# Last stage with rows loaded in place and the norm two steps behind; the experts' narrow product in column groups

## The chip, the cores and the metric

The kernel runs on one core of one Trainium2 chip. The core has TensorE (PE in the profile: matmuls, with its weight loads as PEld), VectorE (DVE), ScalarE (ACT), GpSimd (POOL), SyncE (SP, which here only issues DMAs) and 16 DMA engines. The metric is the device time of one execution in microseconds (us). 0.2% of it is about 8 us.

## What is computed

A decoder layer of three sublayers, each with a residual and a layer norm, in fp32, for x of 8 batches x 512 tokens x 512. The first two are a self-attention with relative positions and a causal cross-attention. The third is a soft mixture of experts: 16 slots gather from the tokens, each slot passes through its own expert, and the tokens read the slots back. Cut to what matters here:

```python
q = broadcast(slot_query)                       # (8, 16, 512)
o = q + _mha(q, x, x, d_Wq, ...)                # slots gather from tokens
h = _layernorm(o.reshape(8, 16, 1, 512), e_ln_g, e_ln_b)
u = silu(einsum('besd,edf->besf', h, e_W1) + e_b1)      # d = 512, f = 2048, e = 16
g = silu(einsum('besd,edf->besf', h, e_Wg) + e_bg)
y = einsum('besf,efd->besd', u * g, e_W2) + e_b2
o = o + y
out = _mha(x, o, o, c_Wq, c_bq, c_Wk, c_bk, c_Wv, c_bv, c_Wo, c_bo)   # tokens read 16 slots
x = _layernorm(x + out)
```

## The kernel before

The program is a row of stages, each a function with a block of instruction streams, one for each engine, that wait for each other by semaphores; between stages all engines meet and the stage's semaphores are cleared. The last two stages are touched by the change.

**`experts`** (line 1547). A loop over 16 experts, with batch (8) as the free size of the slots. The weights of an expert are three tiles of 4 MB (`w1`, `wg`, `w2`), each with two buffers; SP issues them in this order, a buffer as soon as the product that read it is done (`d_wide`, `d_narrow`). PE does for each of `w1` and `wg` a wide product: 16 matmuls with 32 columns of slots as stationary and 512 columns of weights moving, four at a time into four groups of 32 partitions of `ps_u` (line 1618). The result is copied, transposed (1626), and DVE and ACT make silu and the product `prod` (1666). The narrow product (1634) has `prod`, 128x8, as stationary and a 128x512 piece of `w2` moving, 16 matmuls that all sum into the same 8 partitions of `ps_y`. DVE copies `ps_y` to `y` (1671), and POOL's queue stores it (1695). Behind the last expert SP also loads what the last stage needs into the buffers that come free: four 1 MB weights into `w1`, four small tiles into `wg`, and there also `xT0` and `x0`, the first batch of tokens, transposed and as rows (1600 to 1606).

**`slots_to_tokens`** (line 1717). Its SP loads `y_all` (1773). DVE clears `kd` and `vd` (1876, 1877), adds `y` and `b2` to `o` (1880, 1882), fills `bq` (1884), and copies `oT` (1886) after PE's transposes of `o`. PE projects `oT` to keys and values (1793), DVE spreads them by heads into `kd` and `vd` (1893), and 18 rounds on PE fold the query weights into the keys and the output weights into the values (1807 to 1814), copied out by DVE and ACT in turn (`fold_out`). So each batch needs only: `scores` (1825, `xT` against `a`), a softmax over 16 slots for each head (`soft_in` 1907 to 1915 on DVE, the exponential 1993 on ACT, `soft_out` 1920 to 1924 on DVE), `turn` (1836, transposes), the copy `pt` (1990 on ACT), `mix` (1845, into `ps_o`), then `norm_in` (1932 adds `ps_o` to `h`, 1937 the statistics), `norm_scales`, `norm_out` and ACT's scaling of `h` (2000), and the store (1763).

Here `h = x + bo` is made by POOL (1974) from the loaded rows `x[j]` into `h[j]`, with two buffers of each. The loop's step `s` does on PE `scores(s)`, `turn(s-1)`, `mix(s-1)`; on DVE `soft_in(s)`, `soft_out(s)`, `norm_in(s-1)` to `norm_out(s-1)`; on SP `load(s+1)` and then `store(s-1)`. `load` issues `xT` and `x` of a batch once `e_scored` and `e_xb` say that the buffers are read. Instructions of an engine run in the order written, so whatever stands behind a wait waits too. `loop` (1116) writes out two steps, a loop of two steps and the last ones.

Of the kernel before, what the change touches and what calls it, by code (L numbers as in the profile page):

```python
# [6 lines left out]
ALU = mybir.AluOpType  # L7
# [4 lines left out]
P = 128  # L12
T4 = S // P
K4 = E // P
H = 16
# [1531 lines left out]
def experts(nc, dr, sem, first, keep):  # L1547


    with ExitStack() as ctx:  # L1550
# [14 lines left out]
        prod = sb("prod", [P, FC, B])  # L1565
# [3 lines left out]
        ps_t = ps("ps_t", [P, 2, 512])  # L1569
        ps_y = ps("ps_y", [B, 512])  # L1570
# [4 lines left out]
        def _(sp):  # L1575
# [20 lines left out]
            weights, xT0, x0, rows, cols = token_tiles(first)  # L1596
# [43 lines left out]
        def _(dve):  # L1640
            def step(e, j):
# [24 lines left out]
                dve.tensor_tensor(prod[:, :, :], act_e[:, 0, :, :], act_e[:, 1, :, :], ALU.mult)\  # L1666
# [4 lines left out]
                dve.tensor_copy(y[32 * j:32 * j + B, :], ps_y[:, :]).then_inc(sem["d_y"], 1)  # L1671

            dve.wait_ge(sem["d_const_in"], 16)
# [28 lines left out]
D_SEMS = ["d_" + n for n in ["sp_waited", "pool_waited", "wide", "narrow", "w1_in1", "wg_in1",  # L1702
# [4 lines left out]
TOKEN_SEMS = ["e_const_in", "e_in0"]  # L1707


def slots_to_tokens(nc, dr, sem, first, keep):  # L1710


    with ExitStack() as ctx:
# [17 lines left out]
        x = [x0, sb("x1", [P, T4, E])]  # L1731
        h = [sb(f"h{i}", [P, T4, E]) for i in range(2)]
# [3 lines left out]
        st = [sb(f"st{i}", [P, T4, 16]) for i in range(2)]  # L1736
# [6 lines left out]
        const_in = 16 * 9  # L1743
        block = ctx.enter_context(nc.Block())

        @block.sync
        def _(sp):
# [3 lines left out]
            def load(b, j):  # L1751
                if not early(b, 2):
                    sp.wait_ge(sem["e_scored"], b - 1)
                    settle()
                    sp.wait_ge(sem["e_xb"], b - 1)
                    settle()
                sp.dma_start(xT[j][:, :, :], dr["x2T"](b)).then_inc(sem[f"e_in{j}"], 16)
                sp.dma_start(x[j][:, :, :], dr["x2"](b)).then_inc(sem[f"e_in{j}"], 16)

            def store(b, j):  # L1760
                sp.wait_ge(sem["e_normed"], b + 1)
                settle()
                sp.dma_start(dr["out"](b), h[j][:, :, :]).then_inc(sem[f"e_stored{j}"], 16)

            def step(s, j):
                if inside(s, -1, B):
                    load(s + 1, 1 - j)
                if inside(s, 1, B):
                    store(s - 1, 1 - j)

            for j in range(2):
                sp.sem_inc(sem[f"e_stored{j}"], 16)
            sp.dma_start(y[:, :], dr["y_all"]).then_inc(sem["e_const_in"], 16)
            loop(sp, B, step, 1)
            for j in range(2):
                sp.wait_ge(sem[f"e_stored{j}"], 8 * B + 16)

# [5 lines left out]
        def _(pe):  # L1783
# [35 lines left out]
            def scores(b, j):  # L1819
                pe.wait_ge(sem[f"e_in{j}"], (b - j) * 16 + 32)  # L1820
                if not early(b, 1):
                    pe.wait_ge(sem["e_biased"], b)
                for t in range(T4):
                    for k in range(K4):
                        mm = pe.matmul(ps_s[:, t // 2, (t % 2) * HS:(t % 2 + 1) * HS], xT[j][:, k, t * P:(t + 1) * P],  # L1825
                                       a[:, k, b, :, :].rearrange("p m n -> p (m n)"),
                                       start=(k == 0), stop=(k == K4 - 1))
                mm.then_inc(sem["e_scored"], 1)

            def turn(b, j):  # L1830
                pe.wait_ge(sem["e_probs"], b + 1)
                if not early(b, 1):
                    pe.wait_ge(sem["e_pt"], b)
                for i in range(2):
                    for t in range(T4):
                        mm = pe.transpose(ps_t[:, i, t * P:(t + 1) * P], sc[j][:, t, i * P:(i + 1) * P], ident[:, :])  # L1836
                mm.then_inc(sem["e_turned"], 1)

            def mix(b, j):
                pe.wait_ge(sem["e_pt"], b + 1)  # L1840
                if not early(b, 1):
# [7 lines left out]
            def step(s, j):  # L1849
                if inside(s, 0, B):  # L1850
                    scores(s, j)
                if inside(s, 1, B):
                    turn(s - 1, 1 - j)
                    mix(s - 1, 1 - j)
# [3 lines left out]
            loop(pe, B, step, 1)  # L1858
# [16 lines left out]
        def _(dve):  # L1875
            dve.memset(kd[:, :, :, :, :].rearrange("p m b h s -> p (m b h s)"), 0.0).then_inc(sem["e_kd"], 1)
            dve.memset(vd[:, :, :, :, :].rearrange("p m b h s -> p (m b h s)"), 0.0).then_inc(sem["e_kd"], 1)
# [4 lines left out]
            dve.tensor_tensor(o[:, :], o[:, :], b2[:, :], ALU.add).then_inc(sem["e_o"], 1)  # L1882
            for m in range(K4):
# [14 lines left out]
            def groups(j):  # L1898
                return sc[j][:, :, :].rearrange("p t (h s) -> p (t h) s", s=NS)

            def soft_in(b, j):

                dve.wait_ge(sem["e_scored"], b + 1)
                if not early(b, 2):
                    dve.wait_ge(sem["e_turned"], b - 1)
                for u in range(2):
                    ins = dve.tensor_tensor(sc[j][:, 2 * u:2 * u + 2, :],
# [251 lines left out]
```

## Time and profile before

| what | value |
|---|---|
| median of 3 timed runs | 3957.59 us (3953.12 to 3958.68) |
| the profiled execution, as timed | 3950.47 us |
| its span in the profile | 3948.8 us |
| experts in it, from the first wide product | about 3222 to 3712 us |
| last stage in it | 3712 us to the end |
| PE busy | 3612.2 us (91%) |
| mean of what the DMA engines moved | 277 GB/s |

The rows further down come from the trace of that one execution. Times are us from the span's start. The windows view gives the busy time of each engine in a stretch, the clock that PE was granted (1.00 is 2.4 GHz), the busy share of the DMA engines and what they moved. The timeline gives for each instruction, or several of a line merged, its start, the time it covers, the engine and source line, the tiles written and read, and how long the engine stood idle before it and what released it. The chain is the row of work that ended last, followed back from the last instruction.

### The profile page before, as it was taken

How to read it: one execution, taken by the hardware profiler on the slowest of the kernel's cores; microseconds unless marked ns; L12 is line 12 of the kernel's file. 1: busy time of each engine (PE TensorE's matmuls, PEld its weight loads, DVE VectorE, ACT ScalarE, POOL GpSimd, SP SyncE). 2: the span in 40 equal slices, each digit the busy share in tenths (PEclk: the TensorE clock that was granted, in tenths of full speed). 3: DMA queues.
4: the chain of work that ended last, by engine and by line, in shares of the span. 5: the costliest groups of instructions: out<-in, count | busy, mean ns of one | idle time of the engine just before them, and what ended most of it. 6: DMA issues, size and time to landing. Idle time of an engine off the chain costs nothing. (4 is left out here: it accounts for less than half of the span.)

```text
span 3948.8 us, 65903 instructions
## 1 busy us (share of the span) xinstructions
PE 3612.2 (91%) x19712; PEld 2254.9 (57%) x19712; DVE 2163.0 (55%) x5872; ACT 1769.2 (45%) x3799; POOL 1822.9 (46%) x1652
## 2 busy tenths in 40 slices
PE   6999989999899999999888999999899977888686
PEld 4777767777677777777444555555455531122253
DVE  4666656666566666666685666666333321111355
ACT  4666556666566666665355555555121210000033
POOL 3666656666566666665326777777211000000112
PEclk8999999999999999999999999999999988889898
DMA  7999999999899999999783322222444249999623
GB/s 281 386 386 382 379 367 361 385 381 382 339 392 385 376 388 380 384 383 390 227 251 109 94 84 84 84 84 74 156 165 160 88 168 415 417 418 415 246 93 120
DMA packets 429721, 1091.94 MB, mean 277 GB/s; under 512 B 25152, under 2 KB 107584, under 8 KB 380224
## 3 DMA queue, kind: packets, MB, share of 16 engines
q1 hardware_dynamic: 412208, 1040.34, 70.5%
q10 hardware_dynamic: 16656, 47.19, 3.1%
q8 instruction: 161, 2.64, 0.3%
q14 instruction: 184, 1.51, 0.1%
q0 software_dynamic: 512, 0.26, 0.0%
HBM read 650.97 MB, written 436.73 MB: 275 GB/s over the span
## 5 line engine op out<-in xcount | busy, mean ns | idle before, releaser
L553 POOL TENSOR_SCALAR a_sc<-a_sc,a_inv 128x512 f32<-128x512 f32 x512 | 822.6, 1607 | 586.2 <-DVE a_inv L496 541.4
L505 DVE COPY a_pt<-a_ps_t 128x512 f32<-128x512 f32 x512 | 353.5, 690 | 545.6 <-PE a_ps_t L237 528.3
L1096 POOL TENSOR_SCALAR b_sc<-b_sc,b_inv 128x128 f32<-128x128 f32 (+3 forms) x512 | 546.3, 1082 | 179.3 <-DVE b_inv L1065 175.9
L375 ACT ACTIVATE a_stage_q<-a_ps_b 128x640 f32<-128x640 f32 x512 | 360.5, 704 | 586.1 <-PE a_ps_b L255 552.3
L1026 ACT ACTIVATE b_sc<-b_sc,b_mx 128x128 f32<-128x128 f32 (+3 forms) x512 | 282.0, 552 | 317.1 <-DVE b_mx L1059 316.8
L489 DVE CUSTOM_DVE_ANT_0 a_sc<-a_ps_s,a_rq 128x512 f32<-128x512 f32 x512 | 353.2, 690 | 76.4 <-PE a_ps_s L227 60.5
L365 ACT ACTIVATE a_sc<-a_sc,a_mx 128x512 f32<-128x512 f32 x512 | 370.0, 723 | 56.0 <-DVE a_mx L489 52.2
L375 ACT ACTIVATE a_stage_k<-a_ps_b 128x640 f32<-128x640 f32 x512 | 357.7, 699 | 0.0
L237 PEld LDWEIGHTS a_ps_t<-a_ident,a_sc 128*128 128x128 f32 x2048 | 247.5, 141 | 146.3 <-issue 140.4
L1059 DVE CUSTOM_DVE_ANT_0 b_sc<-b_ps_s,b_mask 128x128 f32<-128x128 f32 (+3 forms) x512 | 229.5, 488 | 164.8 <-PE b_ps_s L974 161.0
L237 PE MATMUL a_ps_t<-a_ident,a_sc 128*128 128x128 f32 x2048 | 308.9, 273 | 9.2 <-DVE a_pt L505 9.2
L227 PE MATMUL a_ps_s<-a_ident,a_rk 128*128 128x128 f32 x2048 | 307.9, 273 | 0.0
L324 PEld LDWEIGHTS a_ps_o<-a_okv,keep 128*128 128x128 f32 x2048 | 263.3, 191 | 76.4 <-issue 72.0
L1695 POOL DMA_DIRECT2D y<-d_y x16 | 8.5, 532 | 586.6 <-DVE d_y L1671 586.6
L227 PEld LDWEIGHTS a_ps_s<-a_ident,a_rk 128*128 128x128 f32 x2048 | 256.5, 141 | 37.9 <-issue 1.0
L275 PE MATMUL a_ps_c<-a_xT,keep 128*128 128x512 f32 x512 | 256.4, 605 | 22.1 <-DVE a_lo_q L459 12.1
L324 PE MATMUL a_ps_o<-a_okv,keep 128*128 128x128 f32 x2048 | 269.5, 276 | 1.6 <-ACT a_kv L397 1.6
L321 PE MATMUL a_ps_o<-keep,a_okv 128*128 128x512 f32 x512 | 265.8, 606 | 0.4 <-ACT a_kv L400 0.4
L960 PE MATMUL b_ps_q<-b_xT,keep 128*128 128x512 f32 x512 | 259.3, 610 | 6.8 <-PEq L2081 6.8
L225 PE MATMUL a_ps_s<-a_ks,a_qs 128*128 128x512 f32 x512 | 248.1, 485 | 17.4 <-issue 12.3
L1072 DVE COPY b_pt<-b_ps_t 128x128 f32<-128x128 f32 (+3 forms) x512 | 226.9, 485 | 63.7 <-PE b_ps_t L982 63.6
L1249 PE MATMUL f_ps_o<-keep,f_cT 128*128 128x512 f32 x512 | 231.5, 607 | 9.4 <-DMA f_x<-x 9.4
(207 smaller groups left out, 6335.4 us busy)
## 6 DMA issues: line engine op xcount, KB each, us to landing
band_q<-a_stage_q SPq DMA_DIRECT2D x128, 1280.0 KB, 7.0
band_k<-a_stage_k SPq DMA_DIRECT2D x128, 1280.0 KB, 10.0
a_rk<-band_k SPq DMA_DIRECT2D x128, 1024.0 KB, 12.6
a_rq<-band_q SPq DMA_DIRECT2D x256, 512.0 KB, 13.3
d_w<-in_e_W SPq DMA_DIRECT2D x24, 4096.0 KB, 42.8
d_wg<-in_e_Wg SPq DMA_DIRECT2D x16, 4096.0 KB, 28.4
keep<-in_e_W SPq DMA_DIRECT2D x8, 4096.0 KB, 36.1
a_okv<-in_b_wkv ACTq DMA_DIRECT2D x62, 512.0 KB, 7.9
```

Source lines behind the costliest of these rows:

```text
L227: mm = pe.matmul(out[:, r * P:(r + 1) * P], rk[h][:, r, t * P:(t + 1) * P], ident[:, :], is_transpose=True, start=False, stop=(r == T4 - 1))
L237: mm = pe.transpose(ps_t[:, r * P:(r + 1) * P], sc[i % SC][:, r * P:(r + 1) * P], ident[:, :])
L321: mm = pe.matmul(ps_o[:, :], okv[c][:, 0, n, :], oc[:, n, :], start=(n == 0), stop=(n == K4 - 1))
L324: mm = pe.matmul(ps_o[:, n * P:(n + 1) * P], oc[:, k, n * P:(n + 1) * P], okv[c][:, 1, k, :], start=(k == 0), stop=(k == K4 - 1))
L365: act.activation(sc[n][:, :], sc[n][:, :], ACT.Exp, bias=mx[:, n:n + 1], scale=-1.0, accum_out=sm[:, n:n + 1]).then_inc(sem["a_exped"], 1)
L375: act.activation(st[h % 2][:, t, :], src, ACT.Copy).then_inc(sem[f"a_{kind}_staged"], 1)
L489: dve.tensor_tensor_reduce(out=sc[n][:, :], in0=ps_s[i % 2][:, :], in1=rq[rn][:, i % 2, :], scale=-SCALE_A, scalar=BIG, op0=ALU.add, op1=A ...
L505: dve.tensor_copy(pt[:, h % 2, :, t * P:(t + 1) * P], ps_t[:, :].rearrange("p (r n) -> p r n", r=T4)).then_inc(sem["a_pt_out"], 1)
L553: pool.tensor_scalar(sc[n][:, :], sc[n][:, :], inv[:, n:n + 1], None, ALU.mult)\
L960: mm = pe.matmul(ps_q[:, :], wq[:, j % XP, k, :], xT[j // XP][:, k, :], start=(k == 0), stop=(k == K4 - 1))
L1026: act.activation(sc[j % 2][i][:, 0:width(i)], sc[j % 2][i][:, 0:width(i)], ACT.Exp, bias=mx[j % 2][:, i:i + 1], scale=-1.0, accum_out=sm[j ...
L1096: pool.tensor_scalar(sc[j % 2][i][:, 0:width(i)], sc[j % 2][i][:, 0:width(i)], inv[j % 2][:, i:i + 1], None, ALU.mult).then_inc(sem["b_nor ...
```

## The change

In `experts`: `prod` gets 32 columns for each piece, of which 8 are written and the rest are zero from a clear at the beginning. Each matmul of the narrow product writes one of four groups of 32 partitions of a new tile `ps_p`, by its piece `f`. DVE copies `ps_p` to `part`, and one more matmul with `select` (which sums the four groups' rows; made at the beginning from the identity) brings `ps_y`. The two loads of the first batch are taken out of the end of SP's stream.

In `slots_to_tokens`: the first batch is loaded right behind `y_all`. The clears of `kd` and `vd` and the filling of `bq` stand behind the copy of `oT`; POOL waits for `oT_ready` before its first add. Rows are loaded straight into `h`, which has three buffers, and POOL adds `bo` in place; a row load waits for the store that read the buffer. The norm of a batch is done two steps after its scores, in DVE ahead of `soft_in` (`norm_in`, `norm_scales`) and between `soft_in` and `soft_out` (`norm_out`). The turns stand between the two halves of the next batch's scores. All steps are written out.

```diff
@@ experts
-        prod = sb("prod", [P, FC, B])
+        prod = sb("prod", [P, FC, 32])
+        part = sb("part", [P, E])
+        select = sb("select", [P, B])
+        ps_p = ps("ps_p", [P, 512])
@@ sync
-            sp.dma_start(xT0, dr["x2T"](0)).then_inc(sem["e_in0"], 16)
-            sp.dma_start(x0, dr["x2"](0)).then_inc(sem["e_in0"], 16)
@@ tensor
                 if not early(e, 1):
-                    pe.wait_ge(sem["d_y"], e)
+                    pe.wait_ge(sem["d_part"], e)
                 for n in range(FC):
                     c, f = n // FQ, n % FQ
-                    mm = pe.matmul(ps_y[:, :], prod[:, n, :], w2[j][:, 4 * f + c, :], start=(n == 0), stop=(n == FC - 1))
+                    mm = pe.matmul(ps_p[32 * f:32 * f + 32, :], prod[:, n, :], w2[j][:, 4 * f + c, :],
+                                   start=(c == 0), stop=(c == FC // FQ - 1))
                 mm.then_inc(sem["d_narrow"], 1)
+                pe.wait_ge(sem["d_part"], e + 1)
+                if not early(e, 1):
+                    pe.wait_ge(sem["d_y"], e)
+                pe.matmul(ps_y[:, :], select[:, :], part[:, :], start=True, stop=True).then_inc(sem["d_added"], 1)
@@ vector
                 dve.wait_ge(sem["d_narrow"], e + 1)
+                if not early(e, 1):
+                    dve.wait_ge(sem["d_added"], e)
+                dve.tensor_copy(part[:, :], ps_p[:, :]).then_inc(sem["d_part"], 1)
+                dve.wait_ge(sem["d_added"], e + 1)
                 if not early(e, 2):
                     dve.wait_ge(sem[f"d_stored{j}"], (e - j) * 8)
                 dve.tensor_copy(y[32 * j:32 * j + B, :], ps_y[:, :]).then_inc(sem["d_y"], 1)
@@ slots_to_tokens
-        x = [x0, sb("x1", [P, T4, E])]
-        h = [sb(f"h{i}", [P, T4, E]) for i in range(2)]
+        h = [x0, sb("h1", [P, T4, E]), sb("h2", [P, T4, E])]
@@ sync
+            def load_xT(b):
+                if b >= 2:
+                    sp.wait_ge(sem["e_scored"], b - 1)
+                    settle()
+                sp.dma_start(xT[b % 2][:, :, :], dr["x2T"](b)).then_inc(sem[f"e_in{b % 2}"], 16)
+            def load_x(b):
+                if b >= 3:
+                    sp.wait_ge(sem[f"e_stored{b % 3}"], 16 * (b // 3))
+                    settle()
+                sp.dma_start(h[b % 3][:, :, :], dr["x2"](b)).then_inc(sem[f"e_x_in{b % 3}"], 16)
+            def step(s):
+                if s + 1 < B:
+                    load_xT(s + 1)
+                if s >= 2:
+                    store(s - 2)
+                if 1 <= s + 1 < B:
+                    load_x(s + 1)
             sp.dma_start(y[:, :], dr["y_all"]).then_inc(sem["e_const_in"], 16)
+            load_xT(0)
+            load_x(0)
@@ tensor
+            def step(s):
+                if s < B:
+                    scores(s, 0)
+                if 0 <= s - 1 < B:
+                    turn(s - 1)
+                if s < B:
+                    scores(s, 1)
+                if 0 <= s - 1 < B:
+                    mix(s - 1)
@@ vector
-            dve.memset(kd ...)
-            dve.memset(vd ...)
             dve.memset(eps[:, :], EPS).then_inc(sem["e_eps"], 1)
             dve.wait_ge(sem["e_const_in"], const_in)
             ...
+            dve.wait_ge(sem["e_oT_ready"], 1)
+            dve.tensor_copy(oT[:, :, :].rearrange("p k n -> p (k n)"), ps_t[:, 0, :]).then_inc(sem["e_oT"], 1)
+            dve.memset(kd ...)
+            dve.memset(vd ...)
             for m in range(K4):
                 dve.tensor_copy(bq[:, m, :], cols[:, 0, m:m + 1].to_broadcast([P, P])).then_inc(sem["e_bq"], 1)
-            dve.wait_ge(sem["e_oT_ready"], 1)
-            dve.tensor_copy(oT[:, :, :].rearrange("p k n -> p (k n)"), ps_t[:, 0, :]).then_inc(sem["e_oT"], 1)
             ...
+            def step(s):
+                if s >= 2:
+                    norm_in(s - 2)
+                    norm_scales(s - 2)
+                if s < B:
+                    soft_in(s)
+                if s >= 2:
+                    norm_out(s - 2)
+                if s < B:
+                    soft_out(s)
@@ gpsimd
-                    ins = pool.tensor_tensor(h[j][:, t, :], x[j][:, t, :], bo[:, :], ALU.add)
+                    ins = pool.tensor_tensor(h[b % 3][:, t, :], h[b % 3][:, t, :], bo[:, :], ALU.add)
...
             pool.wait_ge(sem["e_const_in"], const_in)
-            loop(pool, B, step, 0)
+            pool.wait_ge(sem["e_oT_ready"], 1)
+            for b in range(B):
+                add(b)
@@ scalar
+            def step(s):
+                if 0 <= s - 1 < B:
+                    turned_out(s - 1)
+                if s >= 2:
+                    std(s - 2)
+                if s < B:
+                    softexp(s)
+                if s >= 2:
+                    norm(s - 2)
```

## Rows read from the trace of the kernel before

**Rows 1.** Windows view: engines' busy us (instructions), PE's clock, DMA share, GB/s; experts.

```profile
3222.00:3712.00 490.00, 391.09 (x1664) 95.58 (x1664) 77.55 (x144) 17.49 (x33) 8.52 (x16) 0.89 1.01 409
```

**Rows 2.** Timeline, the last expert: start, us, engine, line, tiles, [idle before <-releaser].

```profile
3679.80 3.62 PE L1618 MATMUL d_ps_u<-d_wg,d_hs 128*32 128x512 f32 x32
...
3688.28 0.29 DVE L1666 TENSOR_TENSOR d_prod<-d_act_e 128x128 f32<-128x128 f32 x1
...
3690.14 15.96 PE L1634 MATMUL d_ps_y<-keep,d_prod 128*8 128x512 f32 x32 [5.25 <-DMA keep<-in_e_W]
...
3706.14 0.68 DVE L1671 COPY d_y<-d_ps_y 8x512 f32<-8x512 f32 x1 [17.57 <-PE d_ps_y L1634]
3707.43 0.52 POOL L1695 DMA_DIRECT2D y<-d_y  x1 [30.15 <-DVE d_y L1671]
```

**Rows 3.** Timeline, beginning of the last stage.

```profile
3712.86 1.76 DVE L1876 MEMSET e_kd<- 128x2048 f32 x1 [6.04 <-PEq L2081]
...
3715.35 5.83 POOL L1974 TENSOR_TENSOR e_h<-d_wg 128x512 f32<-128x512 f32 x4 [7.40 <-DMA e_y<-y]
3716.69 1.69 DVE L1880 TENSOR_TENSOR d_wg<-d_wg,e_y 128x512 f32<-128x512 f32 x1
...
3719.97 4.94 DVE L1884 COPY e_bq<-d_wg 128x128 f32<-128x128 f32 x4
3720.20 1.09 PE L1787 MATMUL e_ps_t<-d_ident,d_wg 128*128 128x128 f32 x4 [14.09 <-DVE d_wg L1882]
...
3730.89 1.10 DVE L1893 TENSOR_SCALAR e_kd<-e_ps_s,d_wg 32x128 f32<-32x128 f32 x3 [5.37 <-PE e_ps_s L1793]
```

**Rows 4.** Chain that ended last, in order of time: start, us, what; last stage.

```profile
3743.03 1.30 DVE e_a L1896 x2
...
3775.12 7.16 PE e_ps_s L1825 x32
...
3830.01 9.54 DMA d_wg<-x
...
3924.13 9.97 PE e_ps_o L1845 x16
3934.12 2.37 DVE e_h L1932 x2
...
3939.14 0.39 DVE e_st L1944 x4
```

**Rows 5.** Timeline, the first wide product of the experts.

```profile
3222.11 5.89 PE L1618 MATMUL d_ps_u<-d_w,d_hs 128*32 128x512 f32 x32 [2.25 <-DVE d_hs L1644]
```

**Rows 6.** Windows view, the first 3 us of the last narrow product.

```profile
3690.00:3693.00 3.00, 2.85 (x4) 0.51 (x5) 0.00 (x0) 0.00 (x0) 0.00 (x0) 0.50 1.04 384
```

**Rows 7.** Timeline by engine, first steps of the batch loop.

```profile
3790.72 1.04 PE L1836 MATMUL e_ps_t<-d_ident,e_sc 128*128 128x128 f32 x8
3792.87 7.13 PE L1845 MATMUL e_ps_o<-keep,e_pt 128*128 128x512 f32 x16 [1.11 <-ACT e_pt L1990]
...
3810.40 8.80 PE L1845 MATMUL e_ps_o<-keep,e_pt 128*128 x16 [2.61 <-ACT e_pt L1990]
...
3782.31 1.29 DVE L1907 TENSOR_TENSOR e_sc<-e_ps_s,e_cb 128x512 f32<-128x512 f32 x2 [8.80 <-PE e_ps_s L1825]
...
3789.14 1.22 DVE L1924 TENSOR_TENSOR e_sc<-e_sc,e_inv 128x1024 f32<-128x1024 f32 x1
...
3814.50 2.26 DVE L1924 TENSOR_TENSOR e_sc<-e_sc,e_inv 128x1024 f32<-128x1024 f32 x1
...
3806.42 2.93 ACT L2000 ACTIVATE e_h<-e_h,e_st 128x512 f32<-128x512 f32 x4 [0.65 <-DVE e_st L1953]
...
3814.41 5.91 POOL L1974 TENSOR_TENSOR e_h<-d_wg 128x512 f32<-128x512 f32 x4 [88.35 <-DMA out<-e_h]
...
3809.45 0.38 SPq L1763 DMA_DIRECT2D out<-e_h  x1
```

**Rows 8.** DMA issues, experts and beginning of the last stage: KB, us to landing.

```profile
e_x<-x SPq DMA_DIRECT2D x1, 1024.0 KB, 7.5
```

More of the change, by code:

```diff
@@ L1595, in _ @@
             loop(sp, NS, step, 0)
-            weights, xT0, x0, rows, cols = token_tiles(first)
+            weights, _, _, rows, cols = token_tiles(first)
             sp.wait_ge(sem["d_wide"], 2 * NS - 3)
@@ L1671, in step @@
                 dve.tensor_copy(y[32 * j:32 * j + B, :], ps_y[:, :]).then_inc(sem["d_y"], 1)
+            dve.memset(prod[:, :, :], 0.0).then_inc(sem["d_set"], 1)
+            dve.wait_ge(sem["d_set"], 1)
+            dve.tensor_reduce(select[:, :], ident[:, :].rearrange("p (f r) -> p r f", f=FQ)[:, 0:B, :], AX.X, ALU.add)\
+               .then_inc(sem["d_set"], 1)
+            dve.wait_ge(sem["d_set"], 2)
             dve.wait_ge(sem["d_const_in"], 16)
@@ L1699, in _ @@
                 pool.wait_ge(sem[f"d_stored{j}"], 8 * NS)
-D_SEMS = ["d_" + n for n in ["sp_waited", "pool_waited", "wide", "narrow", "w1_in1", "wg_in1",
+D_SEMS = ["d_" + n for n in ["set", "part", "added", "sp_waited", "pool_waited", "wide", "narrow", "w1_in1", "wg_in1",
                              "w2_in0", "w2_in1", "hs", "pre", "pre_g", "in", "turned", "prod", "y", "exp",
@@ L1735, in slots_to_tokens @@
         pt = sb("pt", [P, 2, S])
-        st = [sb(f"st{i}", [P, T4, 16]) for i in range(2)]
+        st = [sb(f"st{i}", [P, T4, 16]) for i in range(3)]
         eps = sb("eps", [P, 1])
@@ L1743, in slots_to_tokens, with steps @@
         const_in = 16 * 9
+        def steps(step):
+            for s in range(B + 2):
+                step(s)
         block = ctx.enter_context(nc.Block())
@@ L1817, in _, with scores, turn @@
                 mm.then_inc(sem["e_fold"], 1)
[L1819 to L1823, printed above, removed]
+            def scores(b, half):
+                if half == 0:
+                    pe.wait_ge(sem[f"e_in{b % 2}"], 16 * (b // 2) + 16)
+                    if b:
+                        pe.wait_ge(sem["e_biased"], b)
+                for t in (2 * half, 2 * half + 1):
                     for k in range(K4):
-                        mm = pe.matmul(ps_s[:, t // 2, (t % 2) * HS:(t % 2 + 1) * HS], xT[j][:, k, t * P:(t + 1) * P],
+                        mm = pe.matmul(ps_s[:, t // 2, (t % 2) * HS:(t % 2 + 1) * HS], xT[b % 2][:, k, t * P:(t + 1) * P],
                                        a[:, k, b, :, :].rearrange("p m n -> p (m n)"),
                                        start=(k == 0), stop=(k == K4 - 1))
-                mm.then_inc(sem["e_scored"], 1)
-            def turn(b, j):
+                if half:
+                    mm.then_inc(sem["e_scored"], 1)
+            def turn(b):
                 pe.wait_ge(sem["e_probs"], b + 1)
-                if not early(b, 1):
+                if b:
                     pe.wait_ge(sem["e_pt"], b)
@@ L1847, in mix @@
                 mm.then_inc(sem["e_mixed"], 1)
[L1849 to L1854, printed above, removed]
+            def step(s):
[7 more added lines that the diff above has]
+                    mix(s - 1)
             for j in range(2):
                 pe.wait_ge(sem[f"e_folded{j}"], len(rounds) // 2)
-            loop(pe, B, step, 1)
+            steps(step)
         def fold_out(e, parity, copy):
@@ L1923, in soft_out, with norm_in @@
                 dve.wait_ge(sem["e_inv"], b + 1)
[L1924 removed]
+                dve.tensor_tensor(groups(b), groups(b), inv[:, :].unsqueeze(2).to_broadcast([P, T4 * H, NS]),
                                   ALU.mult).then_inc(sem["e_probs"], 1)
[L1927 removed]
+            def norm_in(b):
                 dve.wait_ge(sem["e_mixed"], b + 1)
@@ L1931, in norm_in @@
                 for u in range(2):
-                    ins = dve.tensor_tensor(h[j][:, 2 * u:2 * u + 2, :], ps_o[u][:, :, :],
-                                            h[j][:, 2 * u:2 * u + 2, :], ALU.add)
+                    ins = dve.tensor_tensor(h[b % 3][:, 2 * u:2 * u + 2, :], ps_o[u][:, :, :],
+                                            h[b % 3][:, 2 * u:2 * u + 2, :], ALU.add)
                 ins.then_inc(sem["e_summed"], 1)
@@ new lines, in norm @@
+            def norm(b):
+                act.wait_ge(sem["e_scales"], b + 1)
+                for t in range(T4):
+                    ins = act.activation(h[b % 3][:, t, :], h[b % 3][:, t, :], ACT.Identity, bias=st[b % 3][:, t, 10:11],
+                                         scale=st[b % 3][:, t, 9:10])
+                ins.then_inc(sem["e_normed"], 1)
+            def step(s):
[7 more added lines that the diff above has]
+                    norm(s - 2)
@@ L2004, in _ @@
             act.wait_ge(sem["e_eps"], 1)
-            loop(act, B, step, 1)
-E_SEMS = ["e_" + n for n in ["sp_waited", "dve_waited", "scored", "xb", "in1", "normed", "stored0", "stored1",
+            steps(step)
+E_SEMS = ["e_" + n for n in ["sp_waited", "dve_waited", "scored", "xb", "in1", "x_in1", "x_in2", "normed", "stored0", "stored1", "stored2",
                              "o", "oT_ready", "oT", "kv_ready", "kd", "bq", "folded0", "folded1", "fold",
```

112 lines of the change are left out of this document (41 added, 71 removed).

## The prediction

> **What bounds the kernel now.** Every number is of one profiled execution: span 3948.8 us, 3950.47 us as timed; the three timed runs have a median of 3957.59. I take the change in the span off the median.
>
> First view: the stretches. The change touches only the last 727 us. In the experts (3222 to 3712) the DMA engines are busy all the time at 409 GB/s [rows 1]: 12.58 MB of weights per expert take about 30 us, and PE's narrow product starts when its `w2` lands [rows 2]. So nothing inside the experts is worth time; only what comes behind the last landing is. That is next [rows 2]: the last `w2` lands at 3690.14, the narrow product takes 15.96, `y` is copied by 3706.82, stored at 3707.43, and the last stage's first DVE instruction starts at 3712.86. All this is serial.
>
> Then the last stage's beginning [rows 3]: DVE clears `kd` and `vd`, adds `y` and `b2` to `o` and fills `bq` before it copies `oT`, so PE's projections start only 4.2 us after its transposes end, and DVE then waits 5.37 us for the first of them. POOL adds `bo` to the first two batches meanwhile, and DVE's adds and copies take as long as POOL's instructions.
>
> Last, the chain of the eight batches [rows 4]. Scores start at 3775.12 and the span ends at 3948.8: 173.7 us. In the chain PE's scores and mixes stand in series with DVE's `h` sums, ACT's norm and, from batch 3 on, a load (9.54 us in the row shown) issued only once the row store before it was let go by the norm. PE is not full; a dependency ring is the bound.
>
> **A. Narrow product in four column groups.** 16 matmuls 128x8 become 16 of 128x32 in four groups, the form of the wide product: as many instructions of 128x512, 3.62 us at the high clock [rows 2], 5.89 us for the first burst of the stage, after a stretch without PE work [rows 5]. The last narrow product started at granted clock 0.50, that is 1.2 GHz, after a stretch without PE work [rows 6]. I take 5.89. It may also start later: the last wide product was held by PE's own work and is now held by `wg`, which lands 10 us (4.19 MB at 409 GB/s) before `w2`, at 3680.0; plus 3.62 to 5.89, plus the 5.15 from its end (3683.42) to the end of `prod` (3688.57) gives 3688.8 to 3691.0 against the landing 3690.14. I take a start of 3690.6 and an end of 3696.5. Added: the copy of `part` (0.68 as `y`'s, 0.04 to start), one matmul of 128x512 with `select` (one of the 16 now takes 15.96/16 = 1.0; I take that, and 2.0 at the low clock, though the burst comes right before it), and `y`'s copy, unchanged, 0.72: 3699.0 against 3706.82. **Gain 7.8**; all at high clock 10.7, all low 6.6. The `prod` clear and `select`'s reduce at the stage's start lie under the weights' stream. The extra DVE and PE waits stand before nothing due: the next `w1` lands 10 us later.
>
> A page of the Trainium skill, "TensorE: Matmul & The Clock Gate", section "HAM oscillation — how this bites in real kernels", speaks against this change: short bursts behind DMA waits all start at the low clock. The clock row agrees for the narrow product. By it the 10.7 of the high clock is out and 7.8 stays.
>
> What is late next: the `c_` weights and rows, 4.98 MB behind `w2`: 3690.1 plus 12.2 at 409 GB/s is 3702.3, a few us more to the semaphore. The stage then starts at 3712.86 - 7.8 = 3705.1 and `y_all` lands at 3707.6 (2.5 after that, as now: 3712.86 to POOL's start at 3715.35 [rows 3]), so these don't bind. `xT(0)` and `x(0)` leave the experts' queue: at no cost, scores need them 56 us later.
>
> **B. Beginning of the last stage,** from `y_all`'s landing. Now: 3715.35 to the first fold at 3743.03, 27.7 us [rows 3, 4]. After: POOL waits for `oT_ready`, so two adds run free. The nearest free SBUF-only `tensor_tensor` is 1.22 for twice the columns [rows 7]: 0.65 each, not 1.69. 1.4 for both, transposes 1.2, `oT` 0.72: 3.3. Then the clears, moved behind it: 3.55; then `bq`, 4.94, still beside POOL: `x(0)` is the third load of the stage, lands 7.5 us after its issue [rows 8] at about 3713, and `bq` starts at 3714.3. Then both spreads, 12.1 as now (3730.89 to 3743.03). 3.3 + 3.55 + 4.94 + 12.1 = 23.9. PE's `wk` projection (5.37) is hidden under clears and `bq` (8.5). **Gain 3.7.** If POOL doesn't hold `bq` (1 us), the projection binds: 3.3 + 5.4 + 12.1 = 20.8, gain 6.8. If the adds are slower, 3.
>
> From the first fold to scores nothing changes (32.1 us); unrolled code fetches more instructions, in the shadow of waits for all I see.
>
> **C. The batch loop.** Moves: norm two steps behind, halves of scores around the turns, rows in three buffers, all unrolled. One step on PE [rows 7]: 3.57 (half of 7.14, scores at 3775.12 [rows 4] less its queueing), turns 0.91, 3.57, mix 7.13: **15.2**. Checks, with 0 at the end of the mix before:
> - Probabilities: DVE needs 8.05 from scores' end to the end of L1924 (3782.31 to 3790.36), begun at -7.1: ready at 0.9, or 1.9 if POOL holds L1924 (2.26 instead of 1.22). The turns start at 3.6. Hidden. ACT's copy `pt` (about 1.1) is under the second half of scores; now it is idle time.
> - The mix needs `ps_o` free: the sum of `h` (2.36) follows the probabilities: 4.3 against 8.1. Hidden.
> - DVE: 8.05 plus norm's 5.4 (sum to variance, 3934.12 to 3939.53 [rows 4]) is 13.5, with POOL's hold on L1915 and L1924 15.5. Just above 15.2.
> - Row buffers, SP's queue: `store(s-2)` waits for the norm at 16 (scores at 8.1, five more to the end of the exponentials, then ACT's four of 2.93 in all), the store lands 5 us later (3809.45 to 3814.41), `load_x(s+1)` waits for it, and `load_xT(s+2)` is queued behind: landed 8 us later at 29, needed at 30.4. The ring is 29.1 us for two steps, 14.6 each.
>
> Three limits at 14.6 to 15.5: I take 15.2 and add 2 us for the loop. From the start of scores: mix(0) ends at 26.9 (7.1, softmax 8.1, turns 0.9, half 3.6, mix 7.1), mix(6) six steps later at 118; then probabilities(7), turn, `pt` and mix end at 128.6; the tail from mix to span end is 14.7 as now (3934.1 to 3948.8). 143.3 + 2 = 145.3. **Gain 28.4.** Better 30.4; worse by 4 if the clock falls in the first and last waits (the last mix took 9.97 now instead of 7.13).
>
> The Trainium skill's page "SBUF — State Buffer", section "Who interferes with whom", says that a DVE instruction with two SBUF inputs and a GpSimd one that reads SBUF exclude each other for a whole instruction. The trace agrees (2.26 against 1.22). By it both L1915 and L1924 can be hit in a step, the 15.5 above; without it 13.5.
>
> **Sum.** 7.8 + 3.7 + 28.4 = 39.9: span 3908.9, median 3957.6 - 39.9 = 3917.7.
>
> **Rivals.**
> 1. *The row buffers bind.* If store, rows and `xT` share the DMA engines (9.54 for the load behind a store instead of 8, store 10 instead of 5, some norm delay), the ring is 36 for two steps, 18 each: 6 x 2.5 = 15 more, 3933. For: `xT` is queued behind the wait for a store. Against: 3 MB a step is half of what DMA moves. 0.12.
> 2. *Better cases together:* `bq` free, experts' end at the high clock, no contention: 39.9 + 3.1 + 2.9 + 2 = 47.9, 3910. Against: `x(0)` lands just then. 0.13.
> 3. *Slower than before.* The same ring at two transfers that each take twice as long and in series: it would have to reach 15.5 + 39.9/6 = 22.2 us a step, 44 a ring, 15 more than the 13 us of store and loads that are in it. Decides from store plus loads over 28 us; the longest now are 5 and 10. Then 3958 and above, say 3968. 0.02.
> 4. *The loop isn't faster though the experts' end is* (a wait I don't see keeps the 17.5 of a step without a load's wait now, mixes at 3792.87 and 3810.40): 6 x 2 = 12 more, 3930. 0.05.
>
> The forecast has 0.68. Range 3908 to 3936: it holds the forecast, 1, 2 and 4 and the ends of A, B and C. A measurement of this kernel tells about 0.2% (8 us) from no change; the gain is five times that: faster 0.97, same 0.01, slower 0.02.
>
> **What would show it.** Right: the last narrow product under 6 us and the stage's first DVE instruction near 3705; `oT` copied 3.3 us after `y_all`, first fold 24 us after it; mixes 15 to 16 us apart, with no PE wait for a DMA; POOL's adds off the path. Wrong: a narrow product of 12 us or more (groups don't overlap), scores waiting for `e_xT` or `d_wg`, mixes 17 us or more apart, PE waiting for the sum of `h` or for probabilities.

## The result: 38.5 us faster

The changed kernel takes 3919.6 us (median of 4 runs, 3914.81 to 3922.1) against 3958.14 before (4 runs). The ratio is 0.9907, interval 0.9893 to 0.9921: 31 to 42 us faster, 0.9%. The forecast was 3918.

The profiled execution has a span of 3917.9 us, only 30.9 less than before's 3948.8, though the timed gain is 38.5. The cause lies ahead of the change: the experts' first load is issued at 3228.86 here and at 3221.78 before, behind identical instructions. Executions differ there by several us, as much as some parts of the change are worth: the last `w2` lands at 3690.1 in the trace of before and at 3698.7 in that of e2 below, whose code up to there is the same. So I measure from that landing as a mark inside each trace; it releases the last narrow product, and the mark is this product's start.

| us from `w2`'s last landing | before | after | gain |
|---|---|---|---|
| `y` copied | 16.7 | 7.9 | 8.8 |
| last stage's first DVE instruction | 22.7 | 16.8 | 5.9 |
| first add of `y_all` (after), POOL's start on `y_all` (before) | 25.2 | 19.5 | 5.8 |
| first fold | 52.9 | 42.9 | 10.0 |
| first scores | 85.0 | 75.0 | 10.0 |
| end of span | 258.7 | 220.5 | 38.2 |

From the first load to the mark before takes 468.4 us and after 468.6: the experts are bound by DMA as before. The windows view answers to [rows 1]; PE is busy for 286 us of the 490 instead of 391, at a lower granted clock (0.81 instead of 0.89):

```profile
3222.00:3712.00 490.00, 286.13 (x1700) 78.52 (x1700) 93.59 (x171) 17.80 (x34) 8.55 (x16) 0.81 1.00 405
```

Timeline of the changed kernel, last expert and beginning of the last stage; the answers to [rows 2] and [rows 3]:

```profile
3686.60 5.34 PE L1619 MATMUL d_ps_u<-d_wg,d_hs 128*32 128x512 f32 x32 [4.53 <-DMA d_wg<-in_e_Wg]
...
3696.80 0.29 DVE L1672 TENSOR_TENSOR d_prod<-d_act_e 128x128 f32<-128x128 f32 x1
3697.45 5.34 PE L1635 MATMUL d_ps_p<-keep,d_prod 128*32 128x512 f32 x32 [4.04 <-DMA keep<-in_e_W]
...
3702.86 0.69 DVE L1677 COPY d_part<-d_ps_p 128x512 f32<-128x512 f32 x1 [5.77 <-PE d_ps_p L1635]
3703.61 1.02 PE L1641 MATMUL d_ps_y<-d_part,d_select 128*8 128x512 f32 x2 [0.81 <-DVE d_part L1677]
3704.67 0.68 DVE L1681 COPY d_y<-d_ps_y 8x512 f32<-8x512 f32 x1 [1.12 <-PE d_ps_y L1641]
3705.96 0.52 POOL L1710 DMA_DIRECT2D y<-d_y  x1 [29.81 <-DVE d_y L1681]
...
3714.29 0.06 DVE L1905 MEMSET e_eps<- 128x1 f32 x1 [8.94 <-PEq L2124]
...
3716.91 0.69 DVE L1907 TENSOR_TENSOR d_wg<-d_wg,e_y 128x512 f32<-128x512 f32 x1 [2.56 <-DMA e_y<-y]
...
3719.59 0.69 DVE L1911 COPY e_oT<-e_ps_t 128x512 f32<-128x512 f32 x1 [1.27 <-PE e_ps_t L1811]
3720.34 9.63 PE L1817 MATMUL e_ps_s<-e_oT,d_w 128*128 128x128 f32 x64 [0.78 <-DVE e_oT L1911]
...
3720.66 1.76 DVE L1912 MEMSET e_kd<- 128x2048 f32 x1 [0.38 <-issue]
...
3723.10 6.34 POOL L2003 TENSOR_TENSOR d_wg<-d_wg 128x512 f32<-128x512 f32 x4 [16.62 <-DMA d_wg<-x]
3724.48 3.82 DVE L1915 COPY e_bq<-d_wg 128x128 f32<-128x128 f32 x4
...
3740.35 1.29 DVE L1925 COPY e_a<-e_ps_o 128x512 f32<-128x512 f32 x2
```

The product takes 5.34 us instead of 15.96, at a clock that begins low (the row on it stands further down). But DVE's first instruction comes 8.33 us after the issue of `y`'s store (3705.96 to 3714.29) where it was 5.43. The two issue groups, before and after, show why (KB, us to landing):

```profile
y<-d_y POOLq DMA_DIRECT2D x1, 16.0 KB, 2.2
```

```profile
y<-d_y POOLq DMA_DIRECT2D x1, 16.0 KB, 5.5
```

The store lands 3.3 us later, because it now falls in the transfer of the `c_` weights.

The loop, PE's timeline of the changed kernel, from the mix of batch 1 to the mix of batch 2, and the mixes of the last two batches; the answer to PE's rows in [rows 7]:

```profile
3806.77 7.03 PE L1871 MATMUL e_ps_o<-keep,e_pt 128*128 128x512 f32 x16
3813.64 3.62 PE L1850 MATMUL e_ps_s<-e_a,e_xT 128*128 128x256 f32 x16
3817.09 1.04 PE L1862 MATMUL e_ps_t<-d_ident,e_sc 128*128 128x128 f32 x8
3817.96 3.62 PE L1850 MATMUL e_ps_s<-e_a,e_xT 128*128 128x256 f32 x16
3821.42 7.03 PE L1871 MATMUL e_ps_o<-keep,e_pt 128*128 128x512 f32 x16
...
3880.71 7.03 PE L1871 MATMUL e_ps_o<-keep,e_pt 128*128 128x512 f32 x16
3890.66 1.10 PE L1862 MATMUL e_ps_t<-d_ident,e_sc 128*128 128x128 f32 x8 [2.92 <-DVE e_sc L1952]
3893.01 10.12 PE L1871 MATMUL e_ps_o<-keep,e_pt 128*128 128x512 f32 x16 [1.26 <-DVE d_wg L1959]
```

Half the scores, the turns, the other half and the mix follow without a gap. From mix to mix it is 14.65 us, in two of the steps 14.8 and 15.2; in the loop of before it was 17.4 to 20.6 (two of the mixes stand in [rows 7]). At the end of the loop PE waits 2.92 us for the last probabilities, and the last mix takes 10.12 us instead of 7.03.

### The profile page after: what moved, and what is told of

Read it like the earlier page. It is cut to its first block and busy times, and to the rows that moved or that the text cites. A ratio compares the mean times of both kernels' runs of the same rounds, so it can differ in the third digit from the quotient of the medians.

```text
span 3917.9 us, 65917 instructions
## 1 busy us (share of the span) xinstructions
PE 3508.0 (90%) x19744; PEld 2239.2 (57%) x19744; DVE 2177.9 (56%) x5890; ACT 1770.2 (45%) x3799; POOL 1823.9 (47%) x1652
## 5 line engine op out<-in xcount | busy, mean ns | idle before, releaser
L275 PE MATMUL a_ps_c<-a_xT,keep 128*128 128x512 f32 x512 | 256.4, 605 | 21.9 <-DVE a_lo_q L459 12.1
L225 PE MATMUL a_ps_s<-a_ks,a_qs 128*128 128x512 f32 x512 | 248.1, 485 | 17.1 <-issue 11.7
## 6 DMA issues: line engine op xcount, KB each, us to landing
d_w<-in_e_W SPq DMA_DIRECT2D x24, 4096.0 KB, 42.9
```

## The experiments

**1. Each half alone.** e1 takes over only the `experts` function, e2 only the last stage with the first batch's loads in it. Against the changed kernel, e1 has the last stage of before and, at the experts' end,

```diff
+            sp.dma_start(xT0, dr["x2T"](0)).then_inc(sem["e_in0"], 16)
+            sp.dma_start(x0, dr["x2"](0)).then_inc(sem["e_in0"], 16)
```

and e2 has, besides the single `y` copy of before,

```diff
-                    mm = pe.matmul(ps_p[32 * f:32 * f + 32, :], prod[:, n, :], w2[j][:, 4 * f + c, :],
-                                   start=(c == 0), stop=(c == FC // FQ - 1))
+                    mm = pe.matmul(ps_y[:, :], prod[:, n, :], w2[j][:, 4 * f + c, :], start=(n == 0), stop=(n == FC - 1))
```

> Only the narrow product in four column groups is taken over; the last stage and the loads of the first batch are as before. My theory: the product falls from 16 to 5.3 us and y is copied 8.8 us earlier after the last landing of w2, but its store now meets the c_ weights on the DMA engines and lands about 2.9 us later after its issue, so the last stage starts 5.9 us earlier. Two more MB are queued behind the c_ weights here, so y_all may land up to 1 us later: 3958 - 5.5 = 3952.5. Rival, the store is not what takes the 2.9 us: the stage starts 8.8 us earlier, 3949.

Measured: 3951.2 against 3954.76, ratio 0.9987 (0.9976 to 0.9998), a gain of 1 to 9 us, which holds both the theory's time and the rival's. The trace decides between them: in it `y` is copied 7.9 us after the mark, the last stage's first load is issued at 17.1 (16.8 with the whole change, 22.3 before), and the span ends at 252.7: 6.0 us gained, as expected; the rival's 8.8 for the stage's start are out.

> The last stage of the change with the experts' narrow product as before (the first batch is loaded in the last stage). My theory: the parts add up. From y_all's landing 4.2 us are gained at the beginning and 28.2 in the loop: 3958 - 32.4 = 3925.6; the store of y issued after a 16 us product lands in 2 to 3 us, on free DMA engines. Rival, the parts overlap (the loads at the beginning are late without the experts' gain, or the loop's gain needs it): 3930 or more.

Measured: 3919.59, ratio 0.9905 (0.9888 to 0.9921), 37.6 us by the timed runs; in the trace 227.2 from the mark, 31.4 us gained. The interval reaches from 31 to 44, so the trace's number decides: 31.4 + 6.0 = 37.4 against 38.2 for both. The parts add up, to within the few us by which the clock shifts such sums: in e2 the first mix came 22.6 us after the first scores instead of 19.7. More than four fifths of the gain are the last stage's.

**2. What in the loop is worth the gain.** e3 undoes the halves of scores:

```diff
                 if s < B:
                     scores(s, 0)
+                    scores(s, 1)
                 if 0 <= s - 1 < B:
                     turn(s - 1)
-                if s < B:
-                    scores(s, 1)
-                if 0 <= s - 1 < B:
                     mix(s - 1)
```

> The changed kernel, but PE does the whole of a batch's scores before the turns of the batch before. My theory: the second half of scores hides ACT's copy of the turned probabilities (1.1 us a step and a few tenths of queueing); without it PE stands idle for it: 7 steps of 1.2 us more, 3919.6 + 8.5 = 3928. Rival, the step is held by the ring of row buffers and transposed tokens or by DVE anyway, at 14.7 to 15.5: at most 3922.

Measured: 3916.94, ratio 0.9897 (0.9878 to 0.9915); loop 146.3 us against 145.5. From the mark to the end it is 218.9 us, 1.5 less than in the changed kernel. Neither of the two: the middle steps do cost 16.0 instead of 14.65, as my theory said, but the ends give it back. The first mix comes 17.8 us after the first scores instead of 19.7, and at the end of the loop (timeline of e3, PE):

```profile
3877.72 7.07 PE L1850 MATMUL e_ps_s<-e_a,e_xT 128*128 128x256 f32 x32
3884.62 1.04 PE L1862 MATMUL e_ps_t<-d_ident,e_sc 128*128 128x128 f32 x8
3886.77 7.13 PE L1871 MATMUL e_ps_o<-keep,e_pt 128*128 128x512 f32 x16 [1.11 <-ACT e_pt L2022]
3895.04 1.09 PE L1862 MATMUL e_ps_t<-d_ident,e_sc 128*128 128x128 f32 x8 [1.13 <-DVE e_sc L1950]
3897.40 7.10 PE L1871 MATMUL e_ps_o<-keep,e_pt 128*128 128x512 f32 x16 [1.26 <-DVE d_wg L1957]
```

The last scores are done before mix(6), not in the middle of the step, so the last probabilities are awaited for 1.13 us instead of 2.92, and the last mix runs at the high clock: 7.10 us instead of 10.12. From the first mix to the mix of batch 6 the halves save 7.6 us (88.6 against 96.2), and at the two ends they give 6.6 of them back. So they are worth nothing here, and e3 is also the run that has the lag of two steps and the three buffers without them: those alone bring the loop to 146.3 us.

e4 does the norm one step behind again, with everything else as changed (SP's order too):

```diff
@@ vector
-                if s >= 2:
-                    norm_in(s - 2)
-                    norm_scales(s - 2)
                 if s < B:
                     soft_in(s)
-                if s >= 2:
-                    norm_out(s - 2)
-                if s < B:
                     soft_out(s)
+                if 0 <= s - 1 < B:
+                    norm_in(s - 1)
+                    norm_scales(s - 1)
+                    norm_out(s - 1)
@@ scalar
-                if s >= 2:
-                    std(s - 2)
                 if s < B:
                     softexp(s)
-                if s >= 2:
-                    norm(s - 2)
+                if 0 <= s - 1 < B:
+                    std(s - 1)
+                    norm(s - 1)
```

> The changed kernel, but DVE and ACT do a batch's norm one step behind its scores instead of two: DVE finishes it in one piece right behind the probabilities, ACT right behind the exponential. SP's order is that of the changed kernel. My theory: DVE's sum of h stands at the same place in DVE's order either way, right behind the mix; only the 0.6 us of scales and 0.7 us of ACT's round trip come into DVE's line, 14.8 us a step, still under PE's 14.65 to 15: 3919 to 3923. The step behind buys next to nothing. Rival, it is what takes the norm off the chain: 17.5 us a step as before, 3938.

Measured: 3946.26, ratio 0.9983 (0.997 to 0.9997); loop 175.1, more than even the rival gave. My theory fell, and all of the loop's gain with the lag. Of the 29.6 us between the two loops 1.7 are the clock's: here the rounds ahead of the loop ran at the full clock (first fold to first scores 30.4 us, not 32.1) and the first mix met the low one (21.4 us after the first scores, not 19.7). From the first fold to the end the lag is worth 27.9 us. The chain of e4 shows what I had left out, one step of it (start, us, what):

```profile
3826.66 7.15 PE e_ps_o L1871 x16
3833.83 2.37 DVE e_h L1959 x2
3836.22 2.48 DVE e_st L1964 x4
3838.84 0.39 DVE e_st L1971 x4
3839.25 0.31 ACT e_st L2015
3839.58 0.19 DVE e_st L1977
...
3841.36 2.21 ACT e_h L2031 x3
3843.56 0.92 ACT e_pt L2022
3844.52 8.85 PE e_ps_o L1871 x16
```

It is a ring: mix, sum of `h`, statistics, square root, scales, ACT's four scalings, ACT's copy of the turned probabilities, next mix. The copy has nothing to do with the norm; it only stands behind it in ACT's order. PE's halves of scores are long done. The place of the sum of `h` in DVE's order, on which I had argued, is the same with either lag; the scales (`norm_out`) do move, and with them ACT's scalings.

e5 leaves the norm one step behind and moves ACT's four scalings alone, behind the next copy (against e4):

```diff
+                if s >= 2:
+                    norm(s - 2)
                 if s < B:
                     softexp(s)
                 if 0 <= s - 1 < B:
                     std(s - 1)
-                    norm(s - 1)
```

> As the run with the norm one step behind (its loop took 175.1 us from the first scores to the end), but ACT does the four scalings of h behind the copy of the next batch's turned probabilities instead of ahead of it; the square root stays ahead. Theory after that run: the lag is worth its 30 us because of ACT's order alone. With the norm ahead of the copy there is a ring mix, sum of h, statistics, square root, scales, four scalings, copy, next mix. With the scalings behind the copy the square root is ready 5.4 us after the mix and the copy follows by 6.6, ahead of the 8 us that PE needs for the halves of scores and the turns: 15 to 15.5 us a step, loop 147 to 151. Rival, DVE's line (norm in one piece ahead of the next softmax, waiting for ACT's square root) is what makes 17.5 to 19: the loop stays over 165.

Measured: 3926.22 in one run; loop 158.2. 17 of the 28 us come back, neither all, as my theory said, nor at most 10, as the rival did. The first mixes are 14.8 apart, later ones 15.8 to 16.9, over the 15.5 I gave. Its chain, one step, names the rest:

```profile
3844.30 2.36 DVE d_wg L1959 x2
3846.69 2.48 DVE e_st L1964 x4
...
3849.72 0.31 ACT e_st L2015
...
3850.36 1.38 DVE e_st L1980 x3
...
3851.77 2.93 ACT d_wg L2031 x4
...
3854.72 1.28 ACT L2026
...
3856.01 1.06 ACT e_sc L2026
...
3857.10 1.23 DVE e_sm L1948
```

Now the scalings stand ahead of the next exponential on ACT, with a table load between, and the scales ahead of the next softmax on DVE. The two-step lag puts the scales into DVE's wait for the exponential and the scalings behind it: both rings are gone. So the lag works through the order on ACT, and what is left by e5 through ACT's and DVE's together; how these last 11 of the 28 us divide between the two was not tried.

e6 keeps only the three row buffers: to the edits of e3 and e4 it adds SP's order of before:

```diff
-                if s >= 2:
-                    store(s - 2)
                 if 1 <= s + 1 < B:
                     load_x(s + 1)
+                if 0 <= s - 1 < B:
+                    store(s - 1)
```

> The changed kernel with only the three row buffers of the loop's changes: scores whole, norm one step behind, and the store of a batch behind the next loads in SP's queue, as before. Theory: the ring over ACT stays (17.5 us between mixes), but tokens no longer come with the rows' load behind them, so the 2 to 3 us stalls of every second step go: loop 174 - 8 = 166. Rival, the row loads were most of the cost, and the loop is near 150; or they were none, since the store still holds SP's queue until the norm is done, and it stays at 174.

Measured: 3952.26 in one run; loop 173.6 against 173.7 before. PE waits for tokens for 0.2 us in all, where it waited 8.3 before and [rows 4] shows a 9.54 us load in the chain, and still nothing is gained: the mixes are 17.4 to 19.6 us apart (17.4 to 20.6 before), and PE's waits for ACT's copy are 30 us in sum, where they were 20. The number is the second rival's, but not its reason, since SP's queue held nothing back. Three buffers are what a lag of two steps needs; alone they are no gain, and neither is writing all steps out, which e6 has too.

e12 has a fourth row buffer, with `b % 4` for `b % 3` throughout:

```diff
-        h = [x0, sb("h1", [P, T4, E]), sb("h2", [P, T4, E])]
+        h = [x0, sb("h1", [P, T4, E]), sb("h2", [P, T4, E]), sb("h3", [P, T4, E])]
...
-                if b >= 3:
+                if b >= 4:
```

> The changed kernel with four row buffers instead of three, so that a load waits for the store of two steps ahead of the one it waits for now. Theory: PE waited 0.3 us for transposed tokens in the whole loop, so the ring of row buffers doesn't bind: mixes 14.65 apart still, loop 145 to 146. Rival (the forecast's first): the ring is what holds it near 15, and the loop gains 2 us or more.

Measured: 3921.18 in one run; mixes 14.65 apart, loop 147.9, of which 1.7 stand before the first mix (21.4 against 19.7 us from the first scores; the half of scores ahead of it met the low clock, granted 0.60 there, and took 5.30 us instead of 3.62). PE's wait for tokens is gone. In the changed kernel it was 0.3 us, but 2.8 in the repetition e9:

> The changed kernel once more, beside its variants on the same chip: 220.5 us from w2's last landing to the end, 0.9907 of before, as recorded; runs differ by some 5 us in the stages ahead.

Measured: 3918.5, ratio 0.9901 (0.9884 to 0.9917), 221.8 from the mark. Its PE timeline has the one step in which the ring of row buffers binds by more than 0.4 us:

```profile
3865.90 7.03 PE L1871 MATMUL e_ps_o<-keep,e_pt 128*128 128x512 f32 x16
3875.41 3.72 PE L1850 MATMUL e_ps_s<-e_a,e_xT 128*128 128x256 f32 x16 [2.48 <-DMA e_xT<-x2T]
```

So the forecast's first rival is real but small: with three buffers and the lag a stall of up to 2.5 us in one or two steps of the loop, not 2.5 in each.

**3. The beginning of the last stage.** e7 loads `c_wqT` and `c_wo` in the last stage behind the first rows, with a semaphore of their own, for which PE waits before the first round:

```diff
-            for tile, n in zip(weights, ("c_wk", "c_wv", "c_wqT", "c_wo")):
+            for tile, n in zip(weights[:2], ("c_wk", "c_wv")):
...
             load_x(0)
+            for tile, n in ((wqT, "c_wqT"), (wo, "c_wo")):
+                sp.dma_start(tile, dr[n]).then_inc(sem["e_late_in"], 16)
```

> The changed kernel with two of the 1 MB weights (c_wqT, c_wo) loaded in the last stage, behind the rows of the first batch, instead of at the end of the experts. Theory: y's last store is issued 8.5 us after w2's landing in either, but now finds free DMA engines, since 2.87 MB take 7 us instead of 12: it lands in 2 to 3 us instead of 5.5 and the last stage's first load is issued 13.9 us after w2's landing instead of 16.8; nothing later waits for the two weights. 2.9 us less to the end. Rival, the 2.9 us are in the end of the stage and not in the store: 16.8 stays.

Measured: 3917.66 in one run; the store lands 1.8 us after its issue, and the stage's first load is issued 13.0 us after the mark instead of 16.8:

```profile
y<-d_y POOLq DMA_DIRECT2D x1, 16.0 KB, 1.8
```

3.7 us, a little more than expected. At the end of the span 3.2 of them are left (217.2): the rounds up to the first scores ran 1.7 us faster, the first mix met the low clock and came 1.7 later, and the rest of the loop took 0.5 more. The missing 3 us of the experts' gain are the store behind the weights' transfer.

e8 lets POOL wait until `bq` is filled:

```diff
-            pool.wait_ge(sem["e_oT_ready"], 1)
+            pool.wait_ge(sem["e_bq"], K4)
```

> The changed kernel, but POOL's first add waits until DVE has filled bq. Theory: POOL's instructions hold DVE's four copies (3.8 us); free they take 1 us, and the projection of the keys, ready 5.4 us after oT's copy, then binds at about the same time: 2.5 us less from y_all's landing to the first fold (23.4 to 20.9), and no later cost, since the first sum of h is 70 us away. Rival, the copies are slow by themselves (broadcast source): no change.

Measured: 3917.68 in one run. The copies take 0.56 us for all four instead of 3.82, and DVE then waits 1.74 us for the projection; from the add of `y_all` to the first fold 22.0 instead of 23.4 us, a gain of 1.4 where I expected 2.5 (PE's projection binds now: the first spread starts 6.5 us after `oT`'s copy ends, where [rows 3] had 5.4; at the end of the span 3.4 us are gained, but 1.7 of these are rounds that met the full clock):

```profile
3720.62 0.69 DVE L1911 COPY e_oT<-e_ps_t 128x512 f32<-128x512 f32 x1 [1.27 <-PE e_ps_t L1811]
...
3725.51 0.56 DVE L1915 COPY e_bq<-d_wg 128x128 f32<-128x128 f32 x4
3727.81 6.04 DVE L1922 TENSOR_SCALAR e_kd<-e_ps_s,d_wg 32x128 f32<-32x128 f32 x16 [1.74 <-PE e_ps_s L1817]
```

**4. A version that beats both.** e10 does scores whole in the steps of batch 1 and batch 7, in halves between:

```diff
                 if s < B:
                     scores(s, 0)
+                if s in (1, B - 1):
+                    scores(s, 1)
                 if 0 <= s - 1 < B:
                     turn(s - 1)
-                if s < B:
+                if s < B and s not in (1, B - 1):
                     scores(s, 1)
```

> The changed kernel with scores in halves only in the middle steps; in the steps of batch 1 and of batch 7 they are done whole, ahead of the turns. Theory from the run with whole scores everywhere: halves win 1.35 us in each middle step (mixes 14.65 apart against 16.0), but lose 1.9 at the first mix, where PE waits for the first probabilities with half its scores done, and about 4.8 behind mix(6), where the last probabilities come late and the last mix starts at the low clock (10.1 against 7.1). Taking both: loop 145.5 - 1.9 - 4.8 + 1.4 = 140. Rival, the ends cost the same whatever the order: loop 145.

Measured: 3911.04, ratio 0.9889 (0.9872 to 0.9906); loop 141.7, and 214.8 us from the mark. First mix at 17.8, middle steps 14.65 (one 15.1), last interval 10.2; the last mix still took 8.8 us (the clock). 1.7 us short of the expected 140.

e11 takes e7, e8 and e10 together, and one instruction for the four scales:

```diff
-                for t in range(T4):
-                    ins = dve.scalar_tensor_tensor(s_[:, t, 10:11], s_[:, t, 6:7], -1.0, s_[:, t, 9:10],
-                                                   ALU.mult, ALU.mult)
+                ins = dve.scalar_tensor_tensor(s_[:, :, 10:11], s_[:, :, 6:7], -1.0, s_[:, :, 9:10],
+                                               ALU.mult, ALU.mult)
```

> The run before it together with the two weights loaded late, bq filled ahead of POOL's first add, and the four scales of a batch written by one DVE instruction instead of four. Theory: the gains add up, from w2's last landing to the end 220.5 - 3.7 (store of y) - 1.9 (bq) - 5.3 (ends) - 0.5 = 209, 3908 us. Rival, the ends' gain and the earlier beginning overlap in the clock's state: 213.

Measured: 3908.26, ratio 0.9873 (0.9855 to 0.9892), 209.0 us from the mark, against 220.5 and 221.8 in the two profiles of the changed kernel. Its stage's first load is issued at 13.0, the first fold comes at 37.5, the rounds up to the first scores take 33.1 (granted clock 0.90) and the loop 138.4, with a last mix of 7.1. Against the changed kernel the medians of the same comparison differ by 10.2 us (3918.5), but the two intervals (0.9884 to 0.9917 for the changed kernel) overlap a little; that it is faster than before is beyond doubt, that it is faster than the changed kernel rests on the 11.5 to 12.8 us of the traces as well.

## Why the forecast came out, point by point

The terms were 7.8 + 3.7 + 28.4; from the mark they measured 5.9 + 4.2 + 28.2. The places where the time goes were right, and so were the waits that the change removes; that the time came out within 2 us is in part luck, as the terms show.

- **Bound.** Right: experts by DMA, then a serial end; in the loop a ring with ACT's norm in it. The load that I named as its second part was in the chain, but taking it out alone gained nothing (e6), since PE then waited for ACT's copy instead.
- **A, 7.8.** 5.9. Right in the product (8.8 at `y`: 5.34 us where I took 5.89, and no late start, since `prod` was ready 0.36 us before the landing), wrong in the step "so these don't bind". I set the landing of the `c_` weights against `y_all` and not against the 16 KB store, for which I carried over the 5.4 us from store to stage that [rows 2, 3] show on DMA engines about to fall idle. It measured 5.5 us to landing instead of 2.2, and the term 5.9. The clock began low: 25 of the 32 wide products now took 5.1 to 6.6 us, where 31 of them had taken 3.6 before. That is as the Trainium skill's page "TensorE: Matmul & The Clock Gate" has it in the section "HAM oscillation — how this bites in real kernels", from which I quoted. The 3 us around the beginning of the last narrow product (columns as in [rows 6]):

```profile
3697.00:3700.00 3.00, 2.55 (x16) 0.79 (x20) 0.09 (x1) 0.00 (x0) 0.00 (x0) 0.62 1.05 384
```

- **B, 3.7.** 4.2 by the first fold. The adds, transposes and `oT` took 3.4 us (3.3 forecast), the clears 4.2 (3.55), `bq` 3.7 (4.94) and the spreads 12.1. Why `bq` took less than before no run shows; POOL's hold on it is shown by e8. The case with a free `bq` was given as 6.8 and would have been 5.7: the first spread came 6.5 us after `oT`, not 5.4.
- **C, 28.4.** 28.2, by errors that cancel, which was luck. A step takes 14.65, not 15.2 (my four durations sum to 15.18; start to start they are 3.45, 0.87, 3.46 and 6.87, because a matmul's time in the timeline overlaps the next one's) and not 15.5: mix(6) ended at 115.3 instead of 118. From there the last mix took 15.4 us to end instead of 10.6: 3.0 by the low clock, which I had given as a worse case outside the sum, and the rest by probabilities that came 2.9 us behind mix(6) and not 0.9 to 1.9. So it ended at 130.7 instead of 128.6, and these 2.1 us were just what the 2 us that I had added without a cause covered. And the checks say that nothing is late, not why the lag is needed: that ACT's copy stands behind the norm in ACT's order is not in them.
- **Rivals.** 1 appeared, for 0.3 us in one trace of the changed kernel and 2.8 in the other; my ring of 29.1 us for two steps is nearly PE's two steps of 29.3. 2's free `bq` came only by e8, the high clock at the experts' end in no run (the product took 5.3 us in all of them that have the groups). 3 and 4 did not occur.
- What I could not have told from my own text: which of the three moves in the loop brings the gain. I checked that nothing was late with all of them, not what each one frees; e4's expectation shows that I would have given the lag away.

Left open: the clock at the first and last mix. With halves of scores the first mix came 19.7 us after the first scores in some executions and 21.4 in others (22.6 in e2), with nothing in my edits to cause it. Part of it is only moved: in the changed kernel and e9 the rounds ahead took 32.1 us with the first mix at 19.7, in e4, e5, e7 and e12 30.4 with the first mix at 21.4, 51.8 in both cases; only e8 had 30.4 and 19.7. So a loop time can be 1.7 us off by this alone. And how the lag would do with only two row buffers wasn't tried: the third one is what keeps it free of races.

## What to carry to other kernels

Look for a ring not only through data but through the order on one engine: here a copy that PE needed stood behind a norm that nobody waited for, and 17 us came from moving the norm's scalings behind it alone (e5), 28 with the rest of the lag (e4). Check software pipelining at its ends: what wins in the middle of eight steps can lose as much at the first and the last, and may be done differently there. And where a product gets shorter, ask what its small store now falls into.

## What the runs showed of the hardware

- A 16 KB store landed in 1.8 to 2.2 us where the DMA engines were about to fall idle (before, e2, e7, e11) and in 4.9 to 5.8 while they carried weights (after, e1, e3, e8). Its few bytes did not make it quick there.
- Four copies of 128x128 on DVE take 0.56 us in all with POOL idle and 3.8 to 4.9 beside POOL's adds; four scales of one column take 0.37 or up to 2.5, and as a single instruction (e11) 0.17 or 1.0 to 1.3. I had priced the hold on the two big adds only; the tiny scales meet it too.
- One matmul of 128x512 with an 8-column stationary takes 1.02 us alone; 16 of the same length in four column groups take 3.64 at the high clock and 5.34 where the burst begins at the low one; into one group of 8 partitions, begun at the low clock too, they took 15.96 ([rows 2, 6]).
